# Text embedding and Mamba-like text layers on one core: patch tiles loaded at once, the text begun earlier, weight splits moved

## The reference, cut to what matters

```python
# 32 images of 3x96x96 and 32 texts of 77 tokens, D = 256
patches = patchify(x, 16)                                  # (32, 36, 768)
img = concat([cls, patches @ W.T + b]) + pos_enc           # (32, 37, 256)
t = tok_emb[x_txt] + pos_emb[:77]                          # (32, 77, 256)
for l in range(4):                                         # INNER 512, STATE 64
    x_in, x_gate = split(t @ W_in[l].T)
    u  = silu(causal_conv4(x_in))
    hs = scan(h -> 0.95 h + 0.05 (u @ W_B[l].T))
    y  = (hs @ W_C[l].T + D[l] * u) * silu(x_gate)
    t  = layernorm(y @ W_out[l].T + t) * g[l] + b[l]
h = concat([img, t])                                       # (32, 114, 256)
h = h + one attention layer with a bucketed relative bias table
out = layernorm of a mixture of 8 experts (top 2, FFN 512), added to h
```

## Time and profile before

| | us |
|---|---|
| median of three runs (1216.17 to 1218.94) | 1217.46 |
| the profiled execution | 1220.45 |
| its span, from the first to the last instruction | 1218.6 |

### The profile page before, as it was taken

The page is one execution under the profiler, slowest core; times in us unless marked ns, Lnnn a source line. Parts: engine busy times, 40 slices in busy tenths (PEclk is TensorE's granted clock), DMA queues, the critical chain, the costliest instruction groups (busy, mean ns, idle before and its releaser), DMA issues.

```text
span 1218.6 us, 20427 instructions
## 1 busy us (share of the span) xinstructions
PE 1041.6 (85%) x5678; PEld 827.6 (68%) x5679; DVE 727.2 (60%) x1869; ACT 559.6 (46%) x1201; POOL 607.4 (50%) x663
## 2 busy tenths in 40 slices
PE   5578998999899989997597986399999999999920
PEld 4458998999899989997354654166666666666610
DVE  2477887888688868887598797222222222222237
ACT  1335886888588857663255352022222222222224
POOL 5513675677567756776517376323333333333346
PEclk8788999999899989999799695599999999999975
DMA  9352001000100000011264342322222222223254
GB/s 265 99 147 70 2 1 62 1 2 1 61 2 1 2 9 2 10 55 57 73 223 137 108 152 61 83 41 46 43 46 45 43 43 45 46 43 47 42 137 124
DMA packets 55440, 75.42 MB, mean 62 GB/s; under 512 B 10181, under 2 KB 47683, under 8 KB 53317
## 3 DMA queue, kind: packets, MB, share of 16 engines
q1 hardware_dynamic: 32976, 48.79, 13.0%
q0 software_dynamic: 16640, 18.50, 9.2%
q10 hardware_dynamic: 5748, 7.23, 2.1%
HBM read 45.35 MB, written 29.11 MB: 61 GB/s over the span
## 4 chain that ended last, share of the span: by engine, by line
PE 74%; DVE 10%; issue 6%; POOL 4%; DMA 2%; ACT 1%; another core or an unknown queue 1%; DVEq 0%; SPq 0%; POOLq 0%; ACTq 0%
PE bank L1371 19%; PE bank L1121 16%; PE bank L1387 9%; PE bank L1186 9%; PE bank L1181 3%; PE bank L1379 2%; PE bank L1270 2%; PE bank L1083 1%; DVE arena_b L1507 1%; PE bank L1157 1%; PE bank L1149 1%; PE bank L1169 1%; PE bank L1170 1%; PE bank L1273 1%; PE bank L1362 1%
## 5 line engine op out<-in xcount | busy, mean ns | idle before, releaser
L1371 PE MATMUL bank<-arena_a,arena_b 128*128 x512 | 235.2, 602 | 0.8 <-ACT arena_b L852 0.6
L1042 POOL DMA_INDIRECT yrows<-arena_b,dest_i x64 | 99.8, 1559 | 271.5 <-ACT arena_b L864 263.9
L1507 DVE SCALAR_TENSOR_TENSOR arena_b<-bank,sml,arena_b 128x304 f32<-128x304 f32 (+2 forms) x384 | 195.4, 522 | 40.7 <-ACT arena_b L702 37.5
L1121 PE MATMUL bank<-xt_hi,w_hi 128*128 128x308 f32 x512 | 162.9, 318 | 23.0 <-POOL w_lo L923 14.4
L1825 DVE TENSOR_TENSOR arena_b<-bank,arena_b 128x512 f32<-128x512 f32 x64 | 44.2, 691 | 202.7 <-PE bank L1371 202.7
L1371 PEld LDWEIGHTS bank<-arena_a,arena_b 128*128 128x128 f32 x512 | 92.9, 191 | 99.4 <-issue 99.4
L1121 PE MATMUL bank<-xt_hi,w_lo 128*128 128x308 f32 x512 | 159.4, 311 | 0.0
L1121 PE MATMUL bank<-xt_lo,w_hi 128*128 128x308 f32 x512 | 159.0, 310 | 0.0
L945 POOL TENSOR_TENSOR u_halves<-arena_b,u_halves 128x308 fp32r<-128x308 f32 x128 | 110.5, 869 | 56.2 <-ACT arena_b L714 56.2
L939 POOL TENSOR_TENSOR y_lo<-arena_b,y_hi 128x308 fp32r<-128x308 f32 x128 | 108.5, 856 | 45.5 <-ACT y_hi L726 45.1
L1387 PE MATMUL bank<-arena_a,arena_b 128*128 x512 | 121.3, 380 | 1.1 <-DVE arena_b L1837 0.9
(11 more groups left out here) (174 smaller groups left out, 2216.6 us busy)
## 6 DMA issues: line engine op xcount, KB each, us to landing
arena_b<-xrows SPq DMA_DIRECT2D x64, 129.0 KB
arena_a<-in_w_gate SPq DMA_DIRECT2D x4, 1024.0 KB
arena_a<-in_w_up SPq DMA_DIRECT2D x4, 1024.0 KB
arena_a<-in_w_down SPq DMA_DIRECT2D x4, 1024.0 KB
yrows<-arena_b SPq DMA_DIRECT2D x1, 3648.0 KB, 18.3
h_all<-seq SPq DMA_DIRECT2D x8, 448.0 KB
arena_b<-in_patches SPq DMA_DIRECT2D x10, 324.0 KB
w_raw<-in_w_in SPq DMA_DIRECT2D x3, 1024.0 KB
```

Source lines behind the costliest of these rows:

```text
L1042: pool.indirect_dma_start(yrows, bass.IndirectOffsetOnAxis(ap=dest_i[:, k:k + 1], axis=0), f_y[k], None, compute_op=ALU.add).then_inc(y_se ...
L1121: mm = pe.matmul(out_, in_half(w, layer, d, slice(c * P, (c + 1) * P)), x[:, d, cols], start=(k == 0), stop=(k == len(pairs) - 1))
L1371: mm = pe.matmul(bank[q][:, :], x_gt[k][:, d, :], w[:, d, bass.ds(e * FFN, FFN)], start=(d == 0), stop=(d == DC - 1))
L1507: dve.scalar_tensor_tensor(acc[:, :, back_:TXT], x[:, :, 0:TXT - back_], conv_w(s // GROUPS, c, tap), acc[:, :, back_:TXT], ALU.mult, ALU. ...
```

## The change

- The patches' loads: all eleven tiles have a place of their own and are asked for at once, in seven DMAs, right behind the patch weights and the constants; nothing waits for a buffer. SP, PE, DVE and ACT are written out, without loops. Three PSUM banks take the tiles in turn.
- Five groups are embedded and nine tiles made before the text. Tiles 9 and 10 and groups 5, 6 and 7 are put into the text's iterations 1 and 2, on PE, DVE and ACT.
- The bias thirds come behind patch add 0, behind embed 2, and at the end of iteration 0. The table's load moves from ACT's queue to SP's.
- Layer 0's w_lo is made by DVE (split_first), not by POOL.
- The next layer's weights are split in the iterations b%8 = 2 (two pieces), 3 (two), 4 and 5, not 2 to 6.
- In the last layer keep_gain and keep_rows work on step o, in the middle and at the end of POOL's iteration, not on step t near its start.

```diff
@@ placing @@
-        SPLITS_AT = {2: (0,), 3: (1,), 4: (2,), 5: (3,), 6: (4, 5)}
+        SPLITS_AT = {2: (0, 1), 3: (2, 3), 4: (4,), 5: (5,)}
+        PAT_LOADS = ((0,), (1, 2), (3, 4), (5, 6), (7, 8), (9,), (10,))
+        pat_bank = lambda i: bank[3 + i % 3]
@@ SP @@
+            load_patches(0)
+            load_patches(1)
             sp.dma_start(cst[:, :], consts).then_inc(ld_cst, 16)
             sp.dma_start(sml[:, :], small).then_inc(ld_cst, 16)
+            sp.dma_start(tab_s[:, :], rel_bias.partition_broadcast(SEQ)).then_inc(ld_tab, 16)
+            for k in range(2, len(PAT_LOADS)):
+                load_patches(k)
+            for i in range(PT_FULL + 1):
+                sp.wait_ge(pat_ready, i + 1)
...
+            sp.wait_ge(bias_seq, 3 * 3 + 1)
             for layer in range(1, LAYERS):
@@ ACT, head: embedded 0 to 2, split_w_c, w_hi, w_b, embedded 3 and 4 @@
@@ ACT, text_step, behind conv_start(b, 2) @@
+                if i == 1:
+                    for d in range(DC):
+                        embedded(EMBEDDED, d)
@@ ACT, text_step, behind gate_silu(b, 3) @@
+                if i in (1, 2):
+                    for d in range(DC):
+                        embedded(EMBEDDED + i, d)
@@ POOL, head @@
-            split_weights(0, slice(0, W_COLS), SPLITS, SPLITS)
@@ POOL, text_step, behind lower_turned(t, 0) @@
-                if live(t) and not turns(t):
-                    keep_gain(t)
@@ POOL, text_step, behind lower_turned(t, 1) @@
-                if live(t) and not turns(t):
-                    keep_rows(t)
-                if i == STEPS + 1:
-                    norm_ahead(0)
@@ POOL, text_step, behind the weight pieces @@
+                if live(o) and not turns(o):
+                    keep_gain(o)
@@ POOL, text_step, behind lower_half(b, 1) @@
+                if i == STEPS + 1:
+                    norm_ahead(0)
@@ POOL, text_step, last @@
+                if live(o) and not turns(o):
+                    keep_rows(o)
@@ PE, head @@
+            for i in range(3):
+                patch_tile(i)
             pe.wait_ge(ld_cst, 32)
+            for g, later in enumerate(((3, 4), (5,), (6,), (7, 8), ())):
+                turn_embedding(g)
+                for i in later:
+                    patch_tile(i)
-            pe.wait_ge(pat_ready, PT_FULL + 1)
-            pe.wait_ge(act_xt, 2 * GROUPS)
@@ PE, text_step, first @@
+                if i == 1:
+                    patch_tile(PT_FULL - 1)
+                    turn_embedding(EMBEDDED)
+                if i == 2:
+                    pe.wait_ge(pat_ready, PT_FULL + 1)
@@ PE, text_step, behind state_out(o, 2) @@
+                if i == 1:
+                    patch_tile(PT_FULL)
+                    turn_embedding(EMBEDDED + 1)
+                if i == 2:
+                    turn_embedding(EMBEDDED + 2)
+                    pe.wait_ge(act_xt, GROUPS * DC)
@@ DVE, head @@
+            patch_tile(0); bias_part(0); embed(0); patch_tile(1); patch_tile(2); split_input(0)
+            embed(1); patch_tile(3); patch_tile(4); split_input(1); embed(2); bias_part(1)
+            patch_tile(5); split_input(2); embed(3); patch_tile(6); split_first(); split_input(3)
+            embed(4); patch_tile(7); patch_tile(8); split_input(4)
@@ DVE, text_step, first @@
+                if i in (1, 2):
+                    embed(EMBEDDED + (i - 1) * 2)
+                if i == 1:
+                    patch_tile(PT_FULL - 1)
@@ DVE, text_step, behind taps(b, 3, 0) @@
+                if i == 1:
+                    split_input(EMBEDDED)
+                    embed(EMBEDDED + 1)
+                    patch_tile(PT_FULL)
@@ DVE, text_step, behind taps(a, 2, 2) @@
-                if i < 2:
-                    bias_part(i + 1)
+                if i == 0:
+                    bias_part(2)
@@ DVE, text_step, last @@
+                if i in (1, 2):
+                    split_input(EMBEDDED + i)
```

More of the change, by code:

```diff
@@ L374, in build @@
         ld_toks = sem("ld_toks")
-        ld_pat = [sem(f"ld_pat{k}") for k in range(2)]
+        ld_pat = [sem(f"ld_pat{k}") for k in range(len(PAT_LOADS))]
+        ld_tab = sem("ld_tab")
         ld_ffn = sem("ld_ffn")
@@ L525, in _, with load_patches @@
             sp.dma_start(tokw_s[:, :, :], tok_w).then_inc(ld_tokw, 16)
-            for k in range(2):
-                sp.dma_start(pat[k][:, :, :], patches[k]).then_inc(ld_pat[k], 16)
+            def load_patches(k):
+                load = PAT_LOADS[k]
+                if load[0] == PT_FULL:
+                    sp.dma_start(pat_tile(PT_FULL), patches_tail).then_inc(ld_pat[k], 16)
+                    return
+                tile, at_ = pat_cols(load[0])
+                sp.dma_start(tile[:, at_:at_ + len(load) * PAT_COLS].rearrange("p (a n) -> p a n", a=len(load)),
+                             patches[load[0]:load[-1] + 1].rearrange("a p c t -> p a (c t)")).then_inc(ld_pat[k], 16)
@@ L683, in split_weights @@
                 act.activation(w_hi[layer % 2][:, part], w_raw[:, part], ACT.Copy).then_inc(split_hi, parts)
-            for d in range(DC):
-                embedded(0, d)
-            with act.Fori(1, GROUPS // 2) as g:
+            for g in range(3):
                 for d in range(DC):
@@ L693, in _ @@
             split_w_b()
-            with act.Fori(GROUPS // 2, GROUPS) as g:
+            for g in range(3, EMBEDDED):
                 for d in range(DC):
@@ L1469, in bias_part, with split_first @@
                     c.done()
-            patch_tile(0, 0, PT, 0)
+            def split_first():
+                dve.wait_ge(split_hi, SPLITS)
+                dve.tensor_tensor(w_lo[0][:, :], w_raw[:, :], w_hi[0][:, :].bitcast(F32), ALU.subtract).then_inc(split_lo, SPLITS)
+            patch_tile(0)
+            bias_part(0)
             dve.wait_ge(ld_txt_pos, 16 * PIECES)
             dve.wait_ge(zeroed, 2)
-            for i in (2, 3):
-                embed(i - 2, i % 2, 0)
-                patch_tile(i - 1, 1 - i % 2, PT, i // 3)
-                split_input(i - 2)
-            with dve.Fori(2, PT_FULL // 2) as pair:
-                for k in range(2):
-                    embed(pair * 2 + (k - 2), k, pair - 1)
-                    patch_tile(pair * 2 + (k - 1), 1 - k, PT, pair + (k - 1))
-                    split_input(pair * 2 + (k - 2))
-            bias_part(0)
-            patch_tile(PT_FULL - 1, 1, PT, PT_FULL // 2 - 1)
-            patch_tile(PT_FULL, 0, PT_TAIL, PT_FULL // 2)
+            embed(0)
+            patch_tile(1)
+            patch_tile(2)
+            split_input(0)
+            embed(1)
+            patch_tile(3)
+            patch_tile(4)
+            split_input(1)
+            embed(2)
+            bias_part(1)
+            patch_tile(5)
+            split_input(2)
+            embed(3)
+            patch_tile(6)
+            split_first()
+            split_input(3)
+            embed(4)
+            patch_tile(7)
+            patch_tile(8)
+            split_input(4)
             dve.wait_ge(zeroed, ZEROED)
```

110 lines of the change are left out of this document (57 added, 53 removed).

## The result

| | kernel before | changed kernel |
|---|---|---|
| median of 4 runs, us | 1216.82 (1213.38 to 1218.94) | 1176.92 (1171.95 to 1180.64) |
| profiled execution, us (span) | 1220.45 (1218.6) | 1180.64 (1178.8) |
| ratio, 95% interval | | 0.9672 (0.9625 to 0.9719) |
| a second set of runs, median | 1207.00 (7 runs) | 1178.67 (4 runs) |
| ratio, 95% interval | | 0.9759 (0.9715 to 0.9803) |

I forecast 1180, within 1166 to 1196; both sets of the changed kernel lie there. The gain is 40 us in the first set and 28 in the second, and the difference is in the kernel before: the changed kernel took nearly the same in both. Part of what the first profile of the kernel before showed was not there in a later one of the same code.

What follows compares the result with a forecast made beforehand. The text was taken as TensorE-bound, except at layer changes, head, first steps and last layer. 25.6 - 10.6 - 2.5 + 21.6 + 3.5 = 37.6 us off 1220.45 gives 1182.9, less 3.0 for the median: forecast 1180, range 1166 to 1196.

Steps and rivals of the forecast that it cites:

- Layer changes: Where a layer's weights change: earlier split pieces remove the w_lo wait and low clock; gain 21.6 us, from 14 to 22.
- Last layer: Last text layer: moving keep_gain removes waits for row_norm; gain 3.5 us, from 1 to 6.
- Head: Before the first text matmul: its start moves from 75.56 to 50 us; gain 25.6, from 16 to 31.
- piece of 9.65 us: Head's chain before: stall given to another core or unknown queue; added to 50 us for the ceiling of 60.
- First three steps: Start of the text: work moved from the head fits its holes badly; cost 10.6 us, from 3 to 15.
- Next weights: Early text: layer 1's weights, behind the 3.6 MB clear, arrive late and ACT waits; cost 2.5 us, from 0 to 7.
- (a): Rival: head's net 12.5 us falls to about 3, by a returning stall or costlier first steps and weights; 1190 us; chance 0.15.
- (b): Rival: first steps absorb the moved work in PE's idle 11.9 us, weights in time; 1169 us; chance 0.15.
- (c): Rival: doubled split pieces make PE wait for y_lo or u_halves in six steps; 1193 us; chance 0.07.
- (d): Rival: without pauses PE is granted 1.2 GHz for long stretches of text; three such steps make 1223 us; chance 0.03.
- (e): Rival: a layer change still waits, now for the raw weights; rejected in the prediction, no chance given.
- part 5: Early text: layer 1's weights come late behind the 3.6 MB clear, ACT waits and PE sees it; cost 2.5 us.

Runs made afterwards that it cites:

- four old heads: Kernel before profiled again, and with only splits moved, only keeps moved, or head loops written out; first text matmul at 68.73, 65.35, 67.75, 66.77 us.

## Why the prediction was right

Right in the sum: 37.6 us forecast, 39.8 measured between the two profiled executions. By its parts, each against the earlier trace rows and the windows above:

- **Layer changes**, +21.6 forecast. The three stretches give 64.8 - 43.3 = 21.5. Doubled pieces were put at 0.3 in all; the pair of steps that holds them takes 28.94 instead of 28.65, so it is 0.3 in each layer, 0.9 in all.
- **Last layer**, +3.5 forecast, 5.7 measured. Mis-sized: the waits were right, the 2 us of slow matmuls behind them missing.
- **Head**, +25.6 forecast, 25.7 measured, and that is partly luck. The side of the changed kernel was right step by step: tiles 3 and 4 land at 24.8 (23), are done at 32.3 (31), turn(3) follows at 41.9 (42), the text starts at 49.8 (50). The side of the kernel before was one execution with a piece of 9.65 us in it. In four later profiles its head is 65.4 to 68.7, 67.2 on the mean, and the gain 18. Moving w_lo back takes 4.0 of it away again; the working named that collision and gave it no price of its own. I let the piece stand on both sides of the account (in the head of before, and as the ceiling of after) without asking whether it would be there in the next run.
- **First three steps**, -10.6 forecast, -6.8 measured (-7.3 in the second pair of profiles, 46.64 against 39.36). The hole before turn(5) came as described, 6.05 us. Patch add 10 came at 24.35 us into the text, not 27, and the third step ended at 46.8 instead of 50.7. The term that was too large is the 8.4 us for the first state_out: on PE's timeline it starts 34.0 us after the text's start (83.85) where it was 28.7 (104.30), so 5.3 later. The further 7 us that the prediction allowed for operations of VectorE and GpSimd blocking each other in these steps did not show.
- **Next weights**, -2.5 forecast, -5.6 measured. The weights were there 26.3 us after the patch add (26), and ScalarE waited 3.73. PE lost 3.9 for it, and 1.7 more at the low clock; again the part behind the wait was missing. The forecast named the clear ahead of the weights and drew nothing from it; sending the weights first gives 5.3 us back in that pair of steps, 3.9 to 4.8 by the end of the text.

The sum is 25.7 - 6.8 - 5.6 + 21.5 - 0.6 + 5.7 = 39.9, with -0.6 for the doubled pieces of layers 2 and 3 (layer 1's lie in the 5.6); by the ends of the text it is 40.1. Behind the text the two spans differ by 0.3.

Of the rivals, (a) is true in an unforeseen way: where the kernel before is without the piece, the head gives 18 - 7.3 - 5.6 = 5 net, and the whole gain is about 31 with the mean of the four old heads (34.8 against the one profile of the kernel before of that kind) and 28 by the medians. (b) and (c) didn't come: the first steps had no room where it was needed, and the list of PE's waits has none for y_lo or u_halves. (d) didn't: PE's granted clock is 1.00 at all three changes. (e) didn't at any change of layer; the raw weights came late in the first steps instead, as part 5 had it.

## What to carry to other kernels

A hole that the chain gives to no part of the program should be looked for in a second execution before it is counted, on either side. A wait of TensorE costs the wait and the slow matmuls behind it, here 1.7 us for 3.9 and 2.0 for 3.7, so the second belongs in every sum. And where work is moved into another stage, the order on the engine that feeds it decides, not the idle time in sum: with the same work, taking three things out of the way (a bias third, a clear ahead of the next weights, a wait that nobody needed) gave 14 us of text end. The overlap itself gave nothing; it cost 5 to 6 while it made the next weights late, and about 1 without that.

## What the runs showed of the hardware

A GpSimd gather took 4.39 us while VectorE subtracted 128x3072 from SBUF to SBUF (3.34 us), and 0.98 when it didn't; in each of the eight profiles with the subtraction there one gather was that long (2.58 to 4.98 us), while nearly all others took 1.0 to 1.8. The Trainium skill (SBUF — State Buffer, Who interferes with whom) has such a subtraction contend with GpSimd's reads, and infers that it leaves the building of a DMA's descriptors alone; the gather's row here speaks against that second part, though no run tells whether it was the descriptors or the gather's reading of its token numbers from SBUF that had to wait. The other way round, GpSimd's w_lo of 6.65 to 6.71 us stretched VectorE's two-input operations beside it, 0.9 to 1.0 us a pair, to between 4.27 and 7.49. The issue of one DMA on SyncE took 11.58 us when a 3.6 MB transfer stood ahead of it on its queue, and 0.36 when it was sent first. And the same code behind the text took from 620.6 to 633.3 us in one execution or another, 633.3 at a granted clock of 0.87 and 625.1 at 0.89; the clock does not order them all (626.4 at 0.90).
